# A graph attention layer on one core: TensorE takes the second masks' products one step later

## The chip, the cores and the metric

One core of a Trainium2 chip. The metric is the device time of one launch in microseconds (us), the median of the runs. Three runs of the kernel before took 1816.73, 1818.39 and 1822.62 us.

## What is computed

A graph attention layer over 8192 nodes with 128 features and 4 heads of 32, then ELU, a residual and a layer norm:

```
Wh      = (x @ W.T) as (n, 4, 32)
e[n,h,m] = leaky_relu(score_l[n,h] + score_r[m,h], 0.2)
e       = -inf where adj[n,m] + eye == 0
out     = elu(sum over m of softmax(e)[n,h,m] * Wh[m,h,:])
result  = layernorm(x + out)
```

`adj` is an 8192 x 8192 matrix of zeros and ones in fp32, 256 MB, and is read once.

## The kernel before

The exponential of a leaky ReLU is one of two products of a factor of n and a factor of m, by the sign of score_l + score_r. So the kernel makes two masks of bytes for each pair of tiles of m: one of the edges where the sum is not negative (`bmask`), one of the edges where it is (`cmask`), and multiplies each with its own values (`Wh` times the factor of m, split into three bf16 parts side by side, 99 columns).

**Passes and steps.** A pass (`w`, 16 of them) makes the sums of 16 units of 128 rows for one head (passes 0 to 3 are narrow: 8 units for each of two heads). Each pass has 32 steps (`s`), and a step takes two tiles of m. `q = 32 * w + s` counts all 512. In a step TensorE does 32 matmuls with `bmask` and 32 with `cmask` (both line 396), all accumulated in seven PSUM banks (`psum`): the first three and part of the fourth hold the first masks' sums, the rest the second masks'.

**TensorE** (`step`, lines 384 to 421) does for each q: wait for the values and for the first mask, the first masks' 32 products, signal `half_done`; then, in some steps, `turn_block` (lines 357 to 366: 32 matmuls that pack a block of `adj` into bits); then wait for `c_ready`, the second masks' 32 products, signal `mm_done`. `TURNED` says where the blocks are turned: in 14 steps of pass 0, in every second step of passes 1 to 3, at s = 1, 5, 9, ..., 29 of passes 4 to 11 and nowhere after.

**VectorE** does for each q, in program order: `mask_b(q)` (line 695), part of the compares for q + 1 (line 682), and `mask_c(q)` (line 700), which waits for `mm_done` of step q - 3 since `cmask` has 3 buffers. At s = 0 of a pass it adds up the parts of the pass before (line 706): three banks after `half_done` of its last step, four after `mm_done` of its last step. It waits there in program order, ahead of `mask_b` of s = 1. The first products of the new pass wait for the bank that they open (`bank_free`).

**ScalarE** does the other compares (line 488) three steps ahead, up to six first masks being there (`BR`), and the copies of the turned blocks (line 457).

**SyncE** issues all DMAs on one queue, in program order (lines 284 to 313). `adj` comes in blocks of 2 MB, each as two DMAs of 1 MB (`load_block`, line 217) into two buffers. From pass 2 on the values of a step are read from DRAM into a ring of `VR` = 4 (`load_v`, line 248, 99 KB; line 246 in passes 2 and 3, 198 KB). In iteration q SyncE first issues the block for which the last turned block made room, then the values of step q + 3:

```
284:             loaded, turned = 2, AHEAD
285:             for q in range(Q):
287:                 while loaded < NB and loaded - 1 <= turned:
288:                     load_block(loaded)
292:                 if JUST_MADE * STEPS <= q + VR - 1 < Q:
293:                     load_v(q + VR - 1)
294:                 turned += len(TURNED[q])
```

`load_block(n)` waits for `tr_done` of n - 1 blocks, and `load_v(n)` for `mm_done` of step n - 4, which had the same buffer. So after a turn in step t, the order on the queue is values of t + 3, block, values of t + 4.

Of the kernel before, what the change touches and what calls it, by code (L numbers as in the profile page):

```python
# [6 lines left out]
def gat_kernel(nc, x, adj, W, a_l, a_r, out):  # L7
# [12 lines left out]
    STEPS = NT // 2  # L20
# [9 lines left out]
    EVERY_STEPS = STEPS // NG  # L30
# [10 lines left out]
    JUST_MADE = 2  # L41
# [3 lines left out]
    def narrow(w):  # L45
        return UNITS[w][0][2] != UNITS[w][1][2]
# [9 lines left out]
    def turned_at(q):  # L56

        if q < STEPS:
            return [FIRST_TURNS[q]] if q in FIRST_TURNS else []
        if q < 4 * STEPS:  # L60
            return [] if q % 2 else [QUADS + (q - STEPS) // 2]
        n = 4 * QUADS + (q - 4 * STEPS) // 4
        return [n] if q % 4 == 1 and n < NB else []

    TURNED = [turned_at(q) for q in range(Q)]
# [27 lines left out]

    FINISHED = [(1, range(0, SUB)), (3, range(SUB, JC))] + [(4 * c + 3, range(JC)) for c in range(1, NC)]
    ROWS_DONE = [sum(len(js) for _, js in FINISHED[:e]) for e in range(len(FINISHED) + 1)]

    BR, CR, VR, VS, AH = 6, 3, 4, 3, 3
# [10 lines left out]
    with ctx:  # L108
        def sb(name, shape, dt):
            return ctx.enter_context(nc.sbuf_tensor(name, shape, dt))  # L110

        def sem(name):
            return ctx.enter_context(nc.semaphore(name))
# [7 lines left out]
        bmask = sb("bmask", [P, BR, 2, 2, HALF], fp8)  # L121
        cmask = sb("cmask", [P, CR, 2, 2, HALF], fp8)
# [61 lines left out]
        v_prod, v_hi, v_rest, v_mid, v_lo = (sem(s) for s in ("v_prod", "v_hi", "v_rest", "v_mid", "v_lo"))  # L184
# [4 lines left out]
        v_in = [sem(f"v_in{k}") for k in range(VR)]  # L189
        lrow_in, cmp_act, cmp_dve = [sem("lrow_in0"), sem("lrow_in1")], sem("cmp_act"), sem("cmp_dve")  # L190
        b_ready, c_ready, half_done, mm_done, bank_free = (sem(s) for s in ("b_ready", "c_ready", "half_done", "mm_done", "bank_free"))
# [5 lines left out]
        def wait(eng, s, value):  # L197

            if not (isinstance(value, int) and value <= 0):
                eng.wait_ge(s, value)  # L200
# [119 lines left out]
        @block.tensor  # L320
        def _(pe):
            pe.wait_ge(consts, 1)
            pe.wait_ge(w_in, 16)
            nc.tensor.transpose(psum[:, BANKS - 1, 0:P], w_nat[:, :], identf[:, :]).then_inc(w_tr, 1)
            pe.wait_ge(ablk_done, 1)

            nc.tensor.matmul(psum[:, BANKS - 2, 0:2 * H], w_nat[:, :], ablk[:, :], start=True, stop=True).then_inc(wa_done, 1)
            pe.wait_ge(wt_done, 2)

            def turn_x(g):  # L330
                pe.wait_ge(x_in[g % 4], 16 * (g // 4 + 1))
                wait(pe, x_copied, g - 1)
                for j in range(4):
                    last = nc.tensor.transpose(psum[:, g % 2, j * P:(j + 1) * P], xs[:, g % 4, j], identf[:, :])
                last.then_inc(x_tr, 1)

            def project(g):

                pe.wait_ge(x_copied, g + 1)
                wait(pe, wh_copied, 2 * (g - 1))  # L340
                wait(pe, lc_done, g - 1)
                for j in range(4):
                    last = nc.tensor.matmul(psum[:, 2 + 2 * (g % 2) + j // 2, (j % 2) * WH:(j % 2 + 1) * WH], x_t[:, g % 2, j], w_t[:, :],
                                            start=(j % 2 == 0), stop=True, skip_group_check=True)
                last.then_inc(wh_done, 1)

            def turn_l(c):
                pe.wait_ge(lc_done, 4 * (c + 1))
                wait(pe, lrw_done, c)
                nc.tensor.transpose(psum[0:H * JC, BANKS - 1, 0:P], lcols[:, c], identf[:, :]).then_inc(l_tr, 1)  # L350

            def turn_l_back(c):
                pe.wait_ge(l_copied, c + 1)
                nc.tensor.transpose(psum[:, BANKS - 1, P + c * H * JC:P + (c + 1) * H * JC], l_t[0:H * JC, c],
                                    identf[0:H * JC, 0:H * JC]).then_inc(l_back, 1)

            def turn_block(n):

                pe.wait_ge(a_loaded[n % 2], 32 * (n // 2 + 1))
                wait(pe, evac_done, n)  # L360
                for k in range(BITS):
                    for j in range(SUB):
                        block_hi = abuf[:, n % 2, j, k * P:(k + 1) * P].bitcast(bf16)[:, 1::2]
                        last = nc.tensor.matmul(trp[:, j * P // 2:(j + 1) * P // 2], block_hi, pack[:, k], start=(k == 0 and j == 0), stop=True,  # L364
                                                skip_group_check=True)
                last.then_inc(tr_done, 1)

            for g in range(XG + 1):
                if g < XG:
                    turn_x(g)  # L370
                if g > 0:
                    project(g - 1)
                if g > 4 and g % 4 == 1:
                    turn_l(g // 4 - 1)
                if g > 4 and g % 4 == 2:
                    turn_l_back(g // 4 - 1)
                if g == 13:
                    pe.wait_ge(pack_made, 1)
                    turn_block(0)
            turn_block(1)  # L380
            turn_l(NC - 1)
            turn_l_back(NC - 1)

            def step(q):
                w, s = WHERE[q]

                opened = set()

                def product(mask, u, j, b, values):

                    bank, at = PLACE[(b * 2 + u) * SUB + j]
                    opening = s == 0 and bank not in opened
                    if opening:
                        opened.add(bank)
                        wait(pe, bank_free, BANKS * (w - 1) + bank + 1)
                    return nc.tensor.matmul(psum[:, bank, at * S3:(at + 1) * S3], mask[:, j * P:(j + 1) * P], values,  # L396
                                            start=opening, stop=True, skip_group_check=True)

                def values(u, i, b):
                    if w < JUST_MADE:  # L400
                        return vt[:, q // EVERY_STEPS % VS, u, 2 * (s % EVERY_STEPS) + i, b]
                    at = i * VW + b * S3
                    return vring[:, q % VR, u if narrow(w) else 0, at:at + S3]

                ORDER = [(i, u, j) for i in range(2) for u in range(2) for j in range(SUB)]
                if s == 0:
                    ORDER = [(i, u, j) for u in range(2) for j in range(SUB) for i in range(2)]
                if w < JUST_MADE:
                    pe.wait_ge(v_lo, q // EVERY_STEPS + 1)
                else:  # L410
                    pe.wait_ge(v_in[q % VR], 16 * ((q - JUST_MADE * STEPS) // VR + 1))
                pe.wait_ge(b_ready, q + 1)
                for i, u, j in ORDER:
                    last = product(bmask[:, q % BR, u, i], u, j, 0, values(u, i, 0))
                last.then_inc(half_done, 1)
                for n in TURNED[q]:
                    turn_block(n)
                pe.wait_ge(c_ready, q + 1)
                for i, u, j in ORDER:
                    last = product(cmask[:, q % CR, u, i], u, j, 1, values(u, i, 1))  # L420
                last.then_inc(mm_done, 1)

            pe.wait_ge(wh_copied, 2 * XG)
            pe.wait_ge(lc_done, XG)
            pe.wait_ge(lrw_done, NC)
            for q in range(Q):
                step(q)


        @block.scalar  # L430
# [494 lines left out]
```

## Time and profile before

| | |
|---|---|
| median of 3 runs | 1818.39 us |
| profiled execution, its own time | 1823.02 us |
| its span | 1821.2 us |
| VectorE busy | 95% of the span |
| TensorE busy | 91% |
| ScalarE busy | 89% |
| mean granted TensorE clock | 0.986 |

The span runs from the first to the last instruction of the profiled execution. A busy share is a mean over stages with different limits, so the table alone does not say what sets the time. Matmul ends are modelled, so that neighbouring groups overlap by about 0.16 us; from start to start they are exact.

### The profile page before, as it was taken

How to read it: one execution, taken by the hardware profiler on the slowest of the kernel's cores; microseconds unless marked ns; L12 is line 12 of the kernel's file. 1: busy time of each engine (PE TensorE's matmuls, PEld its weight loads, DVE VectorE, ACT ScalarE, POOL GpSimd, SP SyncE). 2: the span in 40 equal slices, each digit the busy share in tenths (PEclk: the TensorE clock that was granted, in tenths of full speed). 3: DMA queues.
4: the chain of work that ended last, by engine and by line, in shares of the span. 5: the costliest groups of instructions: out<-in, count | busy, mean ns of one | idle time of the engine just before them, and what ended most of it. 6: DMA issues, size and time to landing. Idle time of an engine off the chain costs nothing. (4 is left out here: it accounts for less than half of the span.)

```text
span 1821.2 us, 81366 instructions
## 1 busy us (share of the span) xinstructions
PE 1659.8 (91%) x37067; PEld 1627.4 (89%) x37067; DVE 1734.2 (95%) x1928; ACT 1612.2 (89%) x1217; POOL 24.0 (1%) x34
## 2 busy tenths in 40 slices
PE   6788888889898999999999999999999899999993
PEld 6787887889898999999999999999999899999893
DVE  5999999988988999999999999999999999999996
ACT  4989999789779998998989998998989998998981
POOL 0000000000000100000000100000000100000000
PEclk9899999999999999999999999999999999999997
DMA  8995898999997676576666676666662131121111
GB/s 256 342 341 195 308 311 297 367 334 354 355 323 253 208 241 217 181 237 198 216 211 207 200 238 200 211 209 205 220 194 59 31 95 43 36 57 36 32 36 31
DMA packets 241478, 368.12 MB, mean 202 GB/s; under 512 B 12912, under 2 KB 103408, under 8 KB 239600
## 3 DMA queue, kind: packets, MB, share of 16 engines
q1 hardware_dynamic: 241136, 362.92, 60.7%
q8 instruction: 292, 4.78, 1.1%
q14 instruction: 50, 0.41, 0.1%
HBM read 345.57 MB, written 17.30 MB: 199 GB/s over the span
## 5 line engine op out<-in xcount | busy, mean ns | idle before, releaser
L488 ACT ACTIVATE bmask<-lrow,rtab 128x2048 fp8e4<-128x2048 f32 (+1 forms) x936 | 1483.2, 1661 | 33.1 <-DVE cmask L700 24.1
L396 PE MATMUL psum<-vring,bmask 128*128 128x99 bf16 x14336 | 723.4, 208 | 35.5 <-DVE bmask L695 13.2
L396 PE MATMUL psum<-vring,cmask 128*128 128x99 bf16 x14336 | 718.9, 208 | 37.1 <-DVE cmask L700 21.8
L396 PEld LDWEIGHTS psum<-vring,bmask 128*128 128x128 fp8e4 x14336 | 669.0, 97 | 44.8 <-issue 30.6
L396 PEld LDWEIGHTS psum<-vring,cmask 128*128 128x128 fp8e4 x14336 | 661.6, 98 | 51.9 <-DVE cmask L700 30.7
L700 DVE SCALAR_TENSOR_TENSOR cmask<-acache,bmask 128x1024 int32<-128x1024 int32 x512 | 625.0, 1221 | 27.5 <-PE psum L396 20.6
L695 DVE SCALAR_TENSOR_TENSOR bmask<-acache,bmask 128x1024 int32<-128x1024 int32 x512 | 624.2, 1219 | 0.0
L682 DVE TENSOR_SCALAR bmask<-lrow,rtab 128x2048 fp8e4<-128x2048 f32 (+1 forms) x344 | 357.6, 1055 | 0.0
L457 ACT CAST acache<-trp 128x512 int16<-128x512 f32 x128 | 74.0, 578 | 111.4 <-PE trp L364 111.1
L364 PE MATMUL trp<-pack,abuf 128*128 128x64 bf16 x4096 | 144.1, 194 | 15.9 <-issue 11.1
L364 PEld LDWEIGHTS trp<-pack,abuf 128*128 128x128 bf16 x4096 | 132.8, 99 | 17.6 <-issue 12.3
L396 PE MATMUL psum<-vt,bmask 128*128 128x99 bf16 x2048 | 104.2, 209 | 27.7 <-DVE bmask L695 17.4
L396 PEld LDWEIGHTS psum<-vt,bmask 128*128 128x128 fp8e4 x2048 | 95.9, 98 | 28.8 <-issue 28.5
L396 PE MATMUL psum<-vt,cmask 128*128 128x99 bf16 x2048 | 105.1, 209 | 9.1 <-issue 6.8
L396 PEld LDWEIGHTS psum<-vt,cmask 128*128 128x128 fp8e4 x2048 | 96.2, 98 | 12.5 <-issue 7.8
L706 DVE TENSOR_REDUCE acc<-psum 128x165 f32<-128x495 f32 (+1 forms) x112 | 61.4, 620 | 20.6 <-PE psum L396 20.6
L498 ACT ACTIVATE late<-late,nmr,vrs 128x128 f32<-128x128 f32 x64 | 27.2, 486 | 8.7 <-DVE nmr L796 8.7
L439 ACT COPY acache<-psum 128x256 f32<-128x256 f32 x32 | 10.3, 375 | 23.0 <-DVE acache L579 23.0
L493 ACT ACTIVATE late<-late 128x512 f32<-128x512 f32 x16 | 10.0, 628 | 22.1 <-DVE late L756 22.1
L896 POOL TENSOR_TENSOR vrs<-mv,epsc 128x16 f32<-128x16 f32 (+1 forms) x5 | 4.6, 919 | 1747.8 <-DVE mv L790 1747.8
L627 DVE TENSOR_TENSOR late<-vring,vt 128x1056 f32<-128x1056 f32 x16 | 20.1, 1254 | 2.2 <-ACT vt L460 2.2
L619 DVE TENSOR_TENSOR vring<-acache,vv 128x528 f32<-128x528 f32 x32 | 21.1, 702 | 0.8 <-ACT vv L508 0.8
(62 smaller groups left out, 259.9 us busy)
## 6 DMA issues: line engine op xcount, KB each, us to landing
abuf<-in_adj_dram SPq DMA_DIRECT2D x256, 1024.0 KB, 8.4
vring<-v_scratch SPq DMA_DIRECT2D x384, 99.0 KB, 3.1
lrow<-l_scratch SPq DMA_DIRECT2D x16, 1024.0 KB, 7.8
v_scratch<-vt SPq DMA_DIRECT2D x16, 792.0 KB, 11.1
vring<-v_scratch SPq DMA_DIRECT2D x64, 198.0 KB, 8.2
cmask<-in_x_dram SPq DMA_DIRECT2D x16, 256.0 KB, 4.4
late<-in_x_dram SPq DMA_DIRECT2D x16, 256.0 KB, 4.2
out_dram<-late SPq DMA_DIRECT2D x16, 256.0 KB, 3.5
```

What stands on the lines that cost most here:

```text
L364: last = nc.tensor.matmul(trp[:, j * P // 2:(j + 1) * P // 2], block_hi, pack[:, k], start=(k == 0 and j == 0), stop=True, skip_group_chec ...
L396: return nc.tensor.matmul(psum[:, bank, at * S3:(at + 1) * S3], mask[:, j * P:(j + 1) * P], values, start=opening, stop=True, skip_group_c ...
L439: nc.scalar.copy(wh[:, at:at + 3:2].rearrange("p t (h e) -> p t h e", e=E)[:, :, :, 0:DK], both.rearrange("p t (h d) -> p t h d", d=DK)).t ...
L457: nc.scalar.copy(acache[:, c % 2, half, m].bitcast(i16), trp[:, :]).then_inc(evac_done, 1)
L488: last = nc.scalar.activation(to, rows, ACT.Relu, bias=rtab[:, 2 * s + i, H + h:H + h + 1], scale=BIG, saturate=False)
L498: nc.scalar.activation(zz[:, j], zz[:, j], ACT.Identity, bias=nmr[:, j:j + 1], scale=vrs[:, j:j + 1]).then_inc(y_ready, 1)
L619: last = nc.vector.tensor_tensor(v5[:, :, :, b], w4, vb, ALU.mult)
L627: nc.vector.tensor_tensor(vr, vf, dst[:, :, 0:E], ALU.subtract).then_inc(v_rest, 1)
L682: last = nc.vector.tensor_scalar(to, rows, rtab[:, 2 * s + i, h:h + 1], None, ALU.is_ge, saturate=False)
L695: nc.vector.scalar_tensor_tensor(m, adj_words(q), bit_of(q), m, ALU.bitwise_and, ALU.bitwise_and).then_inc(b_ready, 1)
L700: nc.vector.scalar_tensor_tensor(mask_words(cmask[:, q % CR]), adj_words(q), bit_of(q), mask_words(bmask[:, q % BR]), ALU.bitwise_and, ALU ...
L706: nc.vector.tensor_reduce(acc[:, START[b]:START[b] + n], psum[:, b, 0:n * S3].rearrange("p (i s e) -> p i e s", s=3, e=E), AX.X, ALU.add). ...
```

## The change

TensorE's order alone is altered. For each q it does the first masks' products of q, the turned block of q if there is one, and then the second masks' products of q - 1. In the last step of a pass those of q follow at once; in the first step of a pass there are none. No other engine's program is touched. The reset of `opened` is now by pass and bank.

```diff
-            def step(q):
+            opened = set()
+
+            def branch(q, b):
+
                 w, s = WHERE[q]
...
-                if w < JUST_MADE:
-                    pe.wait_ge(v_lo, q // EVERY_STEPS + 1)
+                if b == 0:
+                    if w < JUST_MADE:
+                        pe.wait_ge(v_lo, q // EVERY_STEPS + 1)
+                    else:
+                        pe.wait_ge(v_in[q % VR], 16 * ((q - JUST_MADE * STEPS) // VR + 1))
+                    pe.wait_ge(b_ready, q + 1)
+                    for i, u, j in ORDER:
+                        last = product(bmask[:, q % BR, u, i], u, j, values(u, i))
+                    last.then_inc(half_done, 1)
                 else:
-                    pe.wait_ge(v_in[q % VR], 16 * ((q - JUST_MADE * STEPS) // VR + 1))
-                pe.wait_ge(b_ready, q + 1)
-                for i, u, j in ORDER:
-                    last = product(bmask[:, q % BR, u, i], u, j, 0, values(u, i, 0))
-                last.then_inc(half_done, 1)
-                for n in TURNED[q]:
-                    turn_block(n)
-                pe.wait_ge(c_ready, q + 1)
-                for i, u, j in ORDER:
-                    last = product(cmask[:, q % CR, u, i], u, j, 1, values(u, i, 1))
-                last.then_inc(mm_done, 1)
+                    pe.wait_ge(c_ready, q + 1)
+                    for i, u, j in ORDER:
+                        last = product(cmask[:, q % CR, u, i], u, j, values(u, i))
+                    last.then_inc(mm_done, 1)
...
             for q in range(Q):
-                step(q)
+                branch(q, 0)
+                for n in TURNED[q]:
+                    turn_block(n)
+                if q % STEPS > 0:
+                    branch(q - 1, 1)
+                if q % STEPS == STEPS - 1:
+                    branch(q, 1)
```

## Rows read from the trace of the kernel before

**Rows 1.** The page: span, then busy us and share of each engine.

```profile
span 1821.2 us, 81366 instructions
PE 1659.8 (91%) x37067; PEld 1627.4 (89%) x37067; DVE 1734.2 (95%) x1928; ACT 1612.2 (89%) x1217; POOL 24.0 (1%) x34
```

**Rows 2.** Busy time by stretch: us, engines, granted clock, DMA share, GB/s.

```profile
560.00:1384.00 824.00, 804.13 (x18424) 796.44 (x18422) 815.03 (x832) 764.74 (x475) 10.83 (x4) 1.00 0.65 208
...
313.00:560.00 247.00, 220.53 (x5128) 216.64 (x5127) 214.93 (x255) 202.61 (x211) 3.15 (x2) 0.99 1.01 345
1384.00:1794.00 410.00, 382.78 (x8200) 369.74 (x8197) 407.08 (x423) 360.56 (x204) 4.92 (x2) 1.00 0.17 47
```

**Rows 3.** Waits, 560 to 1384 us: who waited for whom, us, times, longest.

```profile
PE psum L396 <- issue: 6.6, 11, 1.5
...
DVE acc L706 <- PE psum L396: 5.1, 3, 3.0
```

**Rows 4.** Waits over the whole span, those of VectorE for TensorE.

```profile
DVE cmask L700 <- PE psum L396: 20.6, 20, 1.9
DVE acc L706 <- PE psum L396: 20.6, 7, 5.8
```

**Rows 5.** Timeline of TensorE, steps 169 to 173 (pass 5): start, us, what.

```profile
692.64 1.60 PE L396 MATMUL psum<-vring,bmask 128*128 128x99 bf16 x32
...
695.01 1.59 PE L396 MATMUL psum<-vring,cmask 128*128 128x99 bf16 x32
696.44 1.60 PE L396 MATMUL psum<-vring,bmask 128*128 128x99 bf16 x32
...
705.09 1.60 PE L396 MATMUL psum<-vring,bmask 128*128 128x99 bf16 x32
```

**Rows 6.** Timeline of VectorE in the same stretch, the first masks of three steps.

```profile
694.52 1.22 DVE L695 SCALAR_TENSOR_TENSOR bmask<-acache,bmask 128x1024 int32<-128x1024 int32 x1
...
696.92 1.22 DVE L695 SCALAR_TENSOR_TENSOR bmask<-acache,bmask 128x1024 int32<-128x1024 int32 x1
...
700.39 1.22 DVE L695 SCALAR_TENSOR_TENSOR bmask<-acache,bmask 128x1024 int32<-128x1024 int32 x1
```

**Rows 7.** Timeline of SyncE's queue in pass 5: block, values; then a later block.

```profile
695.21 0.94 SPq L217 DMA_DIRECT2D abuf<-in_adj_dram  x2
696.63 8.97 SPq L248 DMA_DIRECT2D vring<-v_scratch  x4
...
720.50 1.52 SPq L217 DMA_DIRECT2D abuf<-in_adj_dram  x2
```

**Rows 8.** Line 217 alone, the block issued at 695.2 us: its two halves.

```profile
DMA to landing us min/median/max: 5.9/7.4/9.0
```

**Rows 9.** Line 248 alone: values issued at 696.6, at 722.1 and from 1385 us on.

```profile
DMA to landing us min/median/max: 8.3/8.3/8.3
...
DMA to landing us min/median/max: 7.4/7.4/7.4
...
DMA to landing us min/median/max: 1.8/1.9/4.3
```

**Rows 10.** Timeline at the end of pass 4, PE and DVE: sums, first products of pass 5.

```profile
661.72 3.83 DVE L706 TENSOR_REDUCE acc<-psum 128x165 f32<-128x495 f32 x7
...
662.70 1.75 PE L396 MATMUL psum<-vring,bmask 128*128 128x99 bf16 x32
...
666.84 1.33 PE L396 MATMUL psum<-vring,bmask 128*128 128x99 bf16 x26 [0.69 <-DVE bmask L695]
```

**Rows 11.** Pass 2: a block on SyncE's queue, and line 246, the values issued at 351.4 us.

```profile
349.96 0.93 SPq L217 DMA_DIRECT2D abuf<-in_adj_dram  x2
...
DMA to landing us min/median/max: 9.1/9.1/9.1
```

**Rows 12.** A gap after which the clock fell, and a stretch with a gap where not.

```profile
1079.63 2.85 PE L396 MATMUL psum<-vring,bmask 128*128 128x99 bf16 x32 [1.95 <-DMA vring<-v_scratch]
...
180.00:183.40 3.40, 0.95 (x21) 0.81 (x18) 3.40 (x5) 3.40 (x4) 0.00 (x0) 1.00 0.00 0
```

More of the change, by code:

```diff
@@ L382, in _, with product @@
             turn_l_back(NC - 1)
-            def step(q):
+            opened = set()
+            def branch(q, b):
                 w, s = WHERE[q]
-                opened = set()
-                def product(mask, u, j, b, values):
+                def product(mask, u, j, values):
                     bank, at = PLACE[(b * 2 + u) * SUB + j]
-                    opening = s == 0 and bank not in opened
+                    opening = s == 0 and (w, bank) not in opened
                     if opening:
-                        opened.add(bank)
+                        opened.add((w, bank))
                         wait(pe, bank_free, BANKS * (w - 1) + bank + 1)
@@ L397, in product, with values @@
                                             start=opening, stop=True, skip_group_check=True)
-                def values(u, i, b):
+                def values(u, i):
                     if w < JUST_MADE:
```

## The prediction

> **What bounds the kernel now.** I read the page first, for the shares: VectorE is busy 95% of the span and TensorE 91% [rows 1]. Both are near the end of what they can give, so stages decide. The busy time by stretch splits them. From 560 to 1384 us (passes 4 to 11, with turned blocks) VectorE is busy 815 of 824 us, 103.0 us for a pass; from 1384 to 1794 us (no blocks) it is busy 407 of 410 us, 102.5 us for a pass. There VectorE sets the time, blocks or not. From 313 to 560 us (passes 2 and 3) the DMA engines are full, share 1.01 [rows 2]. The waits say how little VectorE loses to TensorE: 20.6 us at the second mask and 20.6 us at the sums in the whole span [rows 4], 5.1 us of it between 560 and 1384 us [rows 3].
>
> Then the timeline of one turn, in pass 5, for how close TensorE is behind. TensorE starts the first products of step 169 at 692.64, then turns a block, starts the second products at 695.01, and those of the next step at 696.44: 2.37 us for products and turn, 1.43 us for a half step. Step 173 starts at 705.09, 12.45 us after 169 [rows 5]. VectorE takes 3.47 us for a step with a compare and 2.40 us for one without [rows 6], so for four steps 3 x 3.47 + 2.40 = 12.8 us. TensorE has 0.35 us to spare in four steps.
>
> The queue has as little. The block is issued at 695.21, when the turn ends, the values of step 173 at 696.63, when the second products of 169 end [rows 7]. The block's second half, issued 0.4 us behind its first, lands at 704.6 [rows 8], the values at 696.63 + 8.3 = 704.9 [rows 9], and TensorE starts step 173 at 705.09. Where no block is ahead the same load lands in 1.9 us (median from 1385 us on) [rows 9]. So the values come when the block ahead of them has come, about 9.7 us after it was issued, and TensorE takes them 0.1 to 0.2 us later. That is the edge of a wait, and the change moves both of its ends.
>
> **The change, part by part.**
>
> *Removed: waits inside a step.* TensorE no longer waits for the second mask right behind the first products. TensorE is not the bound there, so this gives nothing. What hides it is VectorE's own work; with that cover gone it would be worth at most VectorE's waits below.
>
> *Moved: the second products, and with them the signal behind which both DMAs stand.* Take a turn in step t. Now: first products of t, turn, block issued at the turn's end; second products of t, values of t + 4 issued. After: first products of t, turn, second products of t - 1. SyncE stands in iteration t until step t - 1 is done, so only then it issues the values of t + 3 and, behind them, the block; the block no longer goes at the turn's end but a half step and one DMA issue later. The values of t + 4 follow one whole step later and still queue behind the block. I keep 9.7 us from the block's issue to their landing. One issue on that queue costs about 0.45 us (0.94 us for the two of a block) [rows 7]. From the block's issue TensorE has 2.87 us of work per step, and until the first products of t + 4 there are six half steps, 6 x 1.43 = 8.6 us, where there were seven after the issue, 10.0 us.
>
> So the block is issued 0.03 + 0.45 us behind the second products, the values land 9.7 us later, 10.2 us in all, and TensorE has 8.6: it waits 1.6 us. This is a loop, because the next block hangs on the turn behind that wait: first products and turn 2.37, second products 1.59 to their end, 0.03 + 0.45 to the block's issue, 9.7 to the landing, 0.05 to the start = 14.2 us for four steps. VectorE's 12.8 no longer decides. Without the move the same loop is 2.37 + about 0.2 + 9.7 + 0.05 = 12.3 us, under 12.8; that is why it costs nothing today.
>
> *Bounds of 9.7.* The later block goes at 720.50 and the values behind it land at 722.1 + 7.4 = 729.5, 9.0 us later [rows 7, 9]. The lower end is 9.0, loop 13.5. Above, the values of t + 3 now go right ahead of the block; their own transfer could push it by 0.3 us: 10.0, loop 14.5. I take 9.7, as nothing of the block's own path changes.
>
> *The pass end.* In the first step of a pass TensorE has only the first products, and the next ones need the mask that VectorE makes after seven sums. Now at the end of pass 4: sums from 661.72 for 3.83 us, first products at 662.70, the next step's at 666.84 after a 0.69 us wait, with the second products between [rows 10]. After, these come later, and TensorE idles some 2 us. When TensorE is late, VectorE waits for the last second products, then makes four sums (4/7 of 3.83 = 2.2 us) and a mask (1.2): with hand-overs 3.7 us from the last products' end to step 1. From the turn in s = 29 to step 1 of the next pass: 2.37 + 5 x 1.43 + 1.59 + 3.7 = 14.8 us.
>
> *Sum for passes 4 to 11.* Seven loops and one end: 7 x 14.2 + 14.8 = 114.2 us for a pass; eight are 914, less one wait of 1.6 because the last two turns have no block left to load: 912. Now they take 824 [rows 2]: +88 us. TensorE has pauses of its own there, 6.6 us [rows 3]; about a third of a loop has no cover, so +2. An idle end of a pass can take the clock down: the first products after the gap at 1079.63 took 2.85 instead of 1.60 us, while 0.95 us of work in 3.4 us left the clock at 1.00 [rows 12]. For eight ends, 0 to 12 us; I take +4.
>
> *Passes 2 and 3*, a block every second step. The block at 349.96 and the values issued at 351.39 that land 9.1 us later give 10.5 us [rows 11]; the loop is 2.37 + 1.59 + 0.48 + 10.5 + 0.05 = 15.0 us per four steps. The measured mean is 247 / 16 = 15.4 us, with full DMA engines [rows 2], but it has quick and slow stretches, and the quick ones lose. Bounds 0 and, if every four steps lost all of the shift of the issue, 1.43 + 0.45 = 1.9 us, +30 (16 x 1.9). I take +10.
>
> *Passes 0 and 1* have no values on the queue: 0 but for the end, where TensorE is behind. With the ends of passes 2 and 3: 1.4 + 1 + 2 us. *Passes 12 to 15* have no blocks; values land in 1.9 us and TensorE's chain of a pass, 63 x 1.43 + 3.7 = 94 us, stays under VectorE's 102.5: 0. *The end*: the last second products come one half step later against the last mask, but the first three sums go ahead of them: +1.
>
> Sum: 88 + 2 + 4 + 10 + 4 + 1 = **+109 us**. The profiled execution took 1823.0 us, 1.8 more than its span, so it would be 1932; it stands 4.6 us above the median, and from 1818.4 I forecast **1927 us**.
>
> A rule of the Trainium skill speaks against the queueing. "DMA: Bandwidth & Descriptors", section "Queues, rings and completion order", says that a later transfer may finish its write before an earlier one, and that completion is not in order per issuing engine. By it the values could land ahead of the block, and the sum would lose its 88. This case's trace shows them 0.3 us behind it, at 704.9 against 704.6.
>
> **The rivals.**
>
> *The values pass the block, or the wait stays covered.* What speaks for it: VectorE has hidden all else. Then only pass ends and small terms remain, 1 to 10 us: 1824. It needs the landing at or below 8.3 us from the block's issue (loop 12.8), and the shortest that I cite is 9.0. Chance 0.08.
>
> *Faster.* The first masks' sums need only the last first products, and these now end a half step before the rest. If the queue holds nothing up, VectorE's waits at the sums shrink by up to 1.43 us in each of seven [rows 4], 10 us, less 1 at the end: 1809. It decides from a landing at 8.3 us or less and pass ends that cost nothing. Chance 0.03.
>
> *The clock.* If each wait of 1.6 us also took TensorE's clock down, products behind it would cost 1.25 us more (2.85 against 1.60) [rows 12]: 55 x 1.25 = 69 on top, 1996. Against it: the emptier stretch at 180 us kept its clock. Chance 0.09.
>
> **How the numbers follow.** The loop has 0.80. With its terms at the low end (9.0: 55 x -0.7 = -39; passes 2 and 3 at 0; clock 0) it gives 1874, at the high end (+0.3 each, +16; passes 2 and 3 +19; clock +8) 1970. A range of 1868 to 1970 holds nearly all of the 0.80. The measurement tells 0.3%, 5.5 us, from no change; the first rival's 0.08 falls about evenly on both sides of that. Faster 0.03, same 0.05, slower 0.92.
>
> **What would show it.** Passes 4 to 11 at about 114 us each and 12 to 15 still at 102; in each; seven waits of TensorE for the values of 1.4 to 1.8 us; the block issued behind a load of values, a half step after the turn; VectorE waiting for TensorE at the second mask. If those passes stay near 103 us, or TensorE's waits are for masks, the step "the values land 9.7 us after the block's issue" is wrong.

## The result and the profile after

The changed kernel takes 1978.5 us (median of 4 runs, 1964.7 to 1981.4) against 1820.4 us (4 runs) for the kernel before: 1.084 times the time, 95% interval 1.081 to 1.087. The forecast was 1927 us within 1868 to 1970. The direction and the mechanism held; the size is 158 us where 109 were forecast, and the time lies 8.5 us above the range.

From the page of the changed kernel: the span, the busy times, the chain that ended last by engine and by line, and two of the costliest groups with the idle time before them.

```profile
span 1979.6 us, 81366 instructions
PE 1706.6 (86%) x37067; PEld 1675.4 (85%) x37067; DVE 1738.6 (88%) x1928; ACT 1614.8 (82%) x1217; POOL 21.8 (1%) x34
...
PE 38%; DMA 29%; DVE 11%; issue 9%; ACT 3%; SPq 1%; DVEq 0%; POOLq 0%; ACTq 0%; POOL 0%
...
L397 PE MATMUL psum<-vring,bmask 128*128 128x99 bf16 x14336 | 742.8, 211 | 178.8 <-DMA vring<-v_scratch 138.0
...
L707 DVE SCALAR_TENSOR_TENSOR cmask<-acache,bmask 128x1024 int32<-128x1024 int32 x512 | 624.8, 1220 | 183.1 <-PE psum L397 178.8
```

VectorE works as long as before (1738.6 against 1734.2 us [rows 1]), so its share falls from 95% to 88%. Two waits of similar size stand out: TensorE before the first masks' products, for the loads of values, 138.0 us; VectorE before the second mask, for TensorE, 178.8 us. They may be one delay seen twice: TensorE is late, and VectorE, with three buffers for the second mask, is held behind it. Which of the two comes first is what the experiments had to show.

The stretches that answer to [rows 2] are passes 4 to 11, passes 12 to 15, and passes 2 and 3. Columns: stretch, its length, busy us of PE, PEld, DVE, ACT, POOL, granted clock, DMA share, GB/s.

```profile
582.00:1545.90 963.90, 843.68 (x18434) 833.96 (x18435) 820.39 (x834) 767.62 (x476) 8.56 (x4) 0.96 0.56 177
...
1542.00:1953.00 411.00, 381.70 (x8202) 374.24 (x8199) 406.81 (x422) 359.11 (x203) 4.92 (x2) 0.99 0.17 47
...
313.00:578.00 265.00, 227.96 (x5133) 223.09 (x5131) 218.52 (x261) 204.85 (x212) 3.15 (x2) 0.96 0.96 320
```

Passes 4 to 11 went from 824 to 964 us, 140 of the 158. Passes 2 and 3 became 16 us longer (262.9 against 246.8 us from their first products to the first products of pass 4; the stretches of the table are cut a little wider). Passes 12 to 15, with the same new order and no blocks, take what they took. The mean granted clock is 0.96 where TensorE waits, in passes 2 to 11. TensorE's and VectorE's waits in passes 4 to 11, in us, times and longest (before, VectorE waited there for TensorE 5.1 us, at the sums [rows 3]):

```profile
DVE cmask L707 <- PE psum L397: 132.1, 70, 5.4
PEld psum L397 <- DMA vring<-v_scratch: 126.8, 62, 3.4
PE psum L397 <- DMA vring<-v_scratch: 111.9, 59, 3.3
```

A loop is the four steps from the first products of a turn's step to those of the next turn's step. One of them, steps 173 to 177 of pass 5, on TensorE (timeline), with the starts that [rows 5] shows for steps 169 to 173, and the turn:

```profile
747.50 1.61 PE L397 MATMUL psum<-vring,bmask 128*128 128x99 bf16 x32 [1.43 <-DMA vring<-v_scratch]
748.96 1.09 PE L364 MATMUL trp<-pack,abuf 128*128 128x64 bf16 x32
749.89 1.59 PE L397 MATMUL psum<-vring,cmask 128*128 128x99 bf16 x32
751.31 1.60 PE L397 MATMUL psum<-vring,bmask 128*128 128x99 bf16 x32
...
761.72 1.61 PE L397 MATMUL psum<-vring,bmask 128*128 128x99 bf16 x32 [1.64 <-DMA vring<-v_scratch]
```

and on SyncE's queue:

```profile
737.51 0.32 SPq L248 DMA_DIRECT2D vring<-v_scratch  x1
737.87 0.99 SPq L217 DMA_DIRECT2D abuf<-in_adj_dram  x2
740.38 11.45 SPq L248 DMA_DIRECT2D vring<-v_scratch  x4
751.87 1.16 SPq L217 DMA_DIRECT2D abuf<-in_adj_dram  x2
```

The second products of step 172 end at 749.89 + 1.59 = 751.48; then the values of step 176 are issued, at 751.51 (the last of the four in the third line), and the block at 751.87, 4.37 us after the start at 747.50. It was 2.57 us (692.64 to 695.21 [rows 5, 7]). From 747.50 to 761.72 are 14.22 us, the 14.2 of the forecast. But the loop before it, from step 169 on, is longer:

```profile
731.95 1.99 PE L397 MATMUL psum<-vring,bmask 128*128 128x99 bf16 x32 [2.12 <-DMA vring<-v_scratch]
733.74 1.91 PE L364 MATMUL trp<-pack,abuf 128*128 128x64 bf16 x32
735.46 2.02 PE L397 MATMUL psum<-vring,cmask 128*128 128x99 bf16 x32
737.32 1.60 PE L397 MATMUL psum<-vring,bmask 128*128 128x99 bf16 x32
```

It takes 15.55 us. The same three groups need 5.37 us (731.95 to 737.32) instead of 3.81 (747.50 to 751.31), 1.56 more, because the clock was at half (granted clock 0.50 in the first row, 1.00 in the second):

```profile
733.00:736.40 3.40, 3.40 (x57) 3.40 (x54) 1.83 (x2) 0.72 (x2) 0.00 (x0) 0.50 0.02 5
747.50:751.00 3.50, 3.50 (x89) 3.50 (x90) 2.38 (x3) 0.91 (x2) 0.00 (x0) 1.00 0.06 14
```

Measured in this way over the 55 loops that lie within a pass and have a block: the mean loop is 15.10 us, 14.50 for the 31 with the full clock and 15.92 for 23 with the half clock (one is between). The block's issue to its last landing takes 9.70 us in the mean (9.22 before), and 8.7 to 11.1 from loop to loop; the values land 0.34 us behind it. So TensorE's wait is not one number either: 1.87 us in the mean, 0.8 to 3.3 from loop to loop.

### The profile page after: what moved, and what is told of

The parts are those of the page before. It is cut to its first block, busy times and chain, and to the rows that moved or that the text cites. A ratio compares the mean times of both kernels' runs of the same rounds, so it can differ in the third digit from the quotient of the medians.

```text
span 1979.6 us, 81366 instructions
## 1 busy us (share of the span) xinstructions
PE 1706.6 (86%) x37067; PEld 1675.4 (85%) x37067; DVE 1738.6 (88%) x1928; ACT 1614.8 (82%) x1217; POOL 21.8 (1%) x34
## 4 chain that ended last, share of the span: by engine, by line
PE 38%; DMA 29%; DVE 11%; issue 9%; ACT 3%; SPq 1%; DVEq 0%; POOLq 0%; ACTq 0%; POOL 0%
PE psum L397 33%; DMA vring<-v_scratch 28%; DVE bmask L702 6%; PE trp L364 5%; ACT bmask L495 3%; DVE acc L713 1%; DVE cmask L707 1%; DMA v_scratch<-vt 1%; DVE vring L626 0%; DVE bmask L689 0%; SPq L217 0%; DVE vt L639 0%; DVE late L634 0%; DVE st L790 0%; ACT late L505 0%
## 5 line engine op out<-in xcount | busy, mean ns | idle before, releaser
L397 PE MATMUL psum<-vring,bmask 128*128 128x99 bf16 x14336 | 742.8, 211 | 178.8 <-DMA vring<-v_scratch 138.0
L397 PEld LDWEIGHTS psum<-vring,bmask 128*128 128x128 fp8e4 x14336 | 685.7, 99 | 199.4 <-DMA vring<-v_scratch 156.1
L707 DVE SCALAR_TENSOR_TENSOR cmask<-acache,bmask 128x1024 int32<-128x1024 int32 x512 | 624.8, 1220 | 183.1 <-PE psum L397 178.8
L397 PEld LDWEIGHTS psum<-vring,cmask 128*128 128x128 fp8e4 x14336 | 670.5, 98 | 6.8 <-issue 6.7
L364 PE MATMUL trp<-pack,abuf 128*128 128x64 bf16 x4096 | 162.6, 203 | 11.9 <-DMA abuf<-in_adj_dram 6.9
L364 PEld LDWEIGHTS trp<-pack,abuf 128*128 128x128 bf16 x4096 | 152.3, 105 | 13.1 <-DMA abuf<-in_adj_dram 7.3
L467 ACT CAST vt<-vring 128x1056 bf16<-128x1056 f32 x16 | 17.8, 1110 | 6.2 <-DVE vring L626 6.2
```

The costliest lines, as they stand in the source:

```text
L467: nc.scalar.copy(vt[:, n % VS].rearrange("p u t b e -> p (u t b) e")[:, :, e:e + E], src).then_inc(done, 1)
L707: nc.vector.scalar_tensor_tensor(mask_words(cmask[:, q % CR]), adj_words(q), bit_of(q), mask_words(bmask[:, q % BR]), ALU.bitwise_and, ALU ...
```

## The experiments

Theory Q: the values of step t + 4, issued behind the block of the turn in step t, come only when the block has come; the block goes later, and TensorE waits. Rival M: what holds the kernel is that the second products, and so the release of the second mask's buffers, come later. Times below are medians; in brackets the ratio to the kernel before with its interval.

**A fifth buffer for the values**, in the changed kernel.

```diff
-    BR, CR, VR, VS, AH = 6, 3, 4, 3, 3
+    BR, CR, VR, VS, AH = 6, 3, 5, 3, 3
```

and SyncE begins these loads in the same step as before. The values of step t + 4 then go ahead of the block, and those behind it are for step t + 5. 

> The changed kernel with five buffers for the values instead of four, nothing else. Theory Q (the values of step t + 4 queue behind the block and TensorE waits for them): with a fifth buffer the same load has two more half steps, 11.5 us against a landing at about 10.5, so the waits for the values go, passes 4 to 11 come back to 102 to 104 us and the whole to 1815 to 1835. Rival M (the second products' signal comes half a step later, and VectorE, with three buffers for the second mask, is held at them: 179 us of such waits stand in the changed kernel's trace): the fifth buffer for the values changes nothing of that, and the time stays near 1978.

1833.3 us (1.006, 1.004 to 1.008). Passes 4 to 11 as one stretch, and the waits in it:

```profile
565.20:1390.50 825.30, 801.94 (x18434) 796.90 (x18435) 816.39 (x833) 765.49 (x476) 10.83 (x4) 1.00 0.65 207
```

```profile
PE psum L399 <- DVE bmask L704: 21.7, 19, 2.0
DVE acc L715 <- PE psum L399: 4.9, 8, 1.0
```

Not one wait for values or at the second mask is left in the list of that stretch, though the second products and their signal stand where they stand in the change, and the second mask has three buffers as before. Rival M falls: VectorE's 178.8 us were the echo. The block is still issued 4.36 us (median) after the start of a loop and still takes 9.70 us to land, so the block's own path is unchanged; only the time that TensorE has is longer.

**SyncE alone, TensorE's order untouched**, in the kernel before: the block waits for the end of the turn's whole step.

```diff
                 wait(sp, tr_done, n - 1)
+                if after is not None:
+                    sp.wait_ge(mm_done, after)
...
-                    load_block(loaded)
+                    load_block(loaded, after=q if 4 * STEPS < q else None)
```

> The kernel before, TensorE's order untouched; only SyncE, from pass 4 on, waits until the turn's whole step is done before it issues the block, so a half step later and right ahead of the values of t + 4. Theory Q: that alone makes the same loop, 2.37 + 1.59 + 0.03 + about 10 + 0.05 = 14.1 us and, with the clock falling in some, 14.5 to 15; passes 4 to 11 take 112 to 120 us, the whole 1900 to 1950, without a product moved. Rival M (the late second products themselves): no change, 1820.

1884.2 us (1.034, 1.032 to 1.037). Not a product was moved, and 53 us of the loss in passes 4 to 11 are here (877 against 824 us). Its waits for values (TensorE's, passes 4 to 11), and the two starts of one loop:

```profile
PE psum L398 <- DMA vring<-v_scratch: 66.3, 59, 1.8
```

```profile
639.49 1.61 PE L398 MATMUL psum<-vring,bmask 128*128 128x99 bf16 x32 [1.83 <-DMA vring<-v_scratch]
...
653.25 1.61 PE L398 MATMUL psum<-vring,bmask 128*128 128x99 bf16 x32 [1.19 <-DMA vring<-v_scratch]
```

13.76 us; the mean of the 55 is 13.73: 4.05 to the block's issue, 9.29 to its landing, 0.33 to the values', 0.05 to the products. The run lies below the 1900 to 1950 that I expected, and the difference to the change's 15.10 says from what: 0.32 is the issue of the values that go ahead of the block in the change, 0.41 the later landing, and the rest, 0.64, the clock, which here never fell (1.00 in the stretch).

```profile
570.10:1447.10 877.00, 807.18 (x18437) 795.72 (x18434) 817.23 (x833) 767.11 (x476) 10.84 (x4) 1.00 0.60 195
```

**Work in the idle time**, for the clock: the change with 24 products into an unused place ahead of each wait.

```diff
             for q in range(Q):
+                if 4 * STEPS <= q < 12 * STEPS and q % 4 == 1 and q % STEPS > 1:
+                    fill(q)
                 branch(q, 0)
```

> The changed kernel, and in passes 4 to 11, just ahead of the wait for the values of s = 5, 9, ..., 29, 24 more products into a place of a bank that nobody reads (about 1.1 us of work where TensorE now idles 1.5 us or more). Its output is that of the changed kernel. Theory Q with the clock term (in 23 of 55 loops TensorE's clock was at half after the wait, and first products, turn and second products took 1.56 us more): idle stretches get short, few of them take the clock down, loops fall from a mean of 15.1 to 14.5 us, the whole by 25 to 36 us to about 1947. Rival W (the long loops come from elsewhere, the clock is only their companion): the same or, for added work, slower, 1978 to 2000.

1955.5 us (1.073, 1.071 to 1.076), 23 us less, with 56 x 1.1 = 62 us of work added. The stretch 4 to 11, and one filled place:

```profile
579.50:1520.00 940.50, 872.43 (x19777) 862.41 (x19778) 819.95 (x833) 769.78 (x477) 8.56 (x4) 0.99 0.57 182
```

```profile
752.28 1.22 PE L430 MATMUL psum<-vring 128*128 128x99 bf16 x24
754.03 1.61 PE L398 MATMUL psum<-vring,bmask 128*128 128x99 bf16 x32 [0.53 <-DMA vring<-v_scratch]
```

The clock stands at 0.99 instead of 0.96 and fell 5 times instead of 25; the mean loop is 14.70 us. TensorE's idle time became shorter, the landing did not (9.74 us). So the clock was a cost of its own: 0.40 us of a loop came back. The 23 us are a little less than the 25 to 36 expected; five falls stay, and the block lands no sooner.

**The new order in passes 4 to 11 alone.**

```diff
-                if q % STEPS > 0:
+                later = 4 * STEPS <= q < 12 * STEPS
+                if later and q % STEPS > 0:
                     branch(q - 1, 1)
-                if q % STEPS == STEPS - 1:
+                if not later or q % STEPS == STEPS - 1:
                     branch(q, 1)
```

> The new order in passes 4 to 11 alone; the others as before. Theory Q: passes 4 to 11 keep their 139 us, passes 0 to 3 give back 15 to 20: 1955 to 1965. Rival E (much of the loss is at starts and ends and in the narrow passes, where TensorE's new order leaves it without second products): under 1930.

1955.3 us (1.074, 1.069 to 1.079). Passes 4 to 11 take 956 us; passes 2 and 3 are back at 245 us. The loss sits where the forecast had it.

**The block first**, at the turn's end and ahead of the values of t + 3.

```diff
+                if w >= 4:
+                    turned += len(TURNED[q])
                 while loaded < NB and loaded - 1 <= turned:
                     load_block(loaded)
...
-                turned += len(TURNED[q])
+                if w < 4:
+                    turned += len(TURNED[q])
```

> The changed kernel with the block, from pass 4 on, issued at the turn's end and ahead of the values of t + 3, as far as it can go forward on the queue. By theory Q it is now the values of t + 3 that stand right behind the block: 2.57 us to the issue, about 9.7 to their landing, then one step of 2.87 us to the next turn's step: a loop of 15.2 us at the full clock, 0.7 longer than the 14.5 of the changed kernel, so passes 4 to 11 get 0 to 40 us slower and the whole 1980 to 2020, with the long waits at s = 4, 8, ... instead of 5, 9, .... If instead the block's late issue as such were the cause, this kernel would be back at 1820 to 1840.

2053.2 us (1.128, 1.125 to 1.130). The block's issue is 2.57 us (median) after the start again, as before the change, and the kernel is the slowest of all. One wait, at s = 16, four steps after the one at s = 12 (762.53 us) and not at 17, and on SyncE's queue the block of the turn at s = 13 with the values behind it:

```profile
779.45 2.26 PE L400 MATMUL psum<-vring,bmask 128*128 128x99 bf16 x32 [2.78 <-DMA vring<-v_scratch]
781.51 2.54 PE L400 MATMUL psum<-vring,cmask 128*128 128x99 bf16 x32
```

```profile
769.54 0.94 SPq L217 DMA_DIRECT2D abuf<-in_adj_dram  x2
770.97 3.21 SPq L248 DMA_DIRECT2D vring<-v_scratch  x2
```

The wait moved to the values that now stand right behind the block, as theory Q has it. The whole lies beyond the 2020 that I gave, by the clock: 0.93 in passes 4 to 11, 40 falls. Loops at full clock take 14.6 us, less than the 15.2 that I worked out; those with a fall take about 17.

**Smaller blocks**, every issue and wait kept.

```diff
+                    if part == 1 and n >= 4 * QUADS + 2:
+                        rows = adj[rows_of(c, half), m * BITS * P:(m + 1) * BITS * P][0:P]
+                        sp.dma_start(abuf[:, n % 2, SUB - 1:SUB], ...).then_inc(a_loaded[n % 2], 16)
+                        continue
```

> The changed kernel; from block 66 on, so in passes 4 to 11, the second DMA of a block brings one tile of rows instead of four (1.25 instead of 2 MB in all), and three row tiles of those blocks keep what the buffer held. All else, every issue and every wait, stands. If the block's transfer is what the values of t + 4 wait for, they land some 2.4 us sooner, within the 8.6 us that TensorE has, the waits go, and the whole is 1830 to 1850. If it is the place of the issue, or the second products' signal, passes 4 to 11 stay near 963 us.

1846.7 us (1.013, 1.012 to 1.015). The block lands 7.10 us after its issue instead of 9.70, passes 4 to 11 (here from 584.3 to 1412.4, first products of their second steps) take 828 us, and few waits for values are left from 561 to 1400 us:

```profile
PE psum L401 <- DMA vring<-v_scratch: 5.2, 4, 2.5
```

The block goes as late as in the change, the signals stand as in the change, and the loss in these passes is gone with a part of the bytes: what the values wait for is the block's transfer. Most of the 25 us that this kernel still loses lie in passes 0 to 3, which the edit does not touch. Its pass 2 took 142 us instead of the change's 134 (from second step to second step); I have no explanation for that.

**The values on a queue of their own**: the same loads, issued by GpSimd.

```diff
-                if JUST_MADE * STEPS <= q + VR - 1 < Q:
-                    load_v(q + VR - 1)
...
+            for q in range(Q):
+                if JUST_MADE * STEPS <= q + VR - 1 < Q:
+                    load_v(q + VR - 1)
```

> The changed kernel with the loads of values issued by GpSimd on its own queue, in the same order and behind the same waits; SyncE then issues the block when the turn ends. Theory Q, as far as it is one queue's order: the values no longer stand behind the block, TensorE does not wait, passes 4 to 11 come back to 102 to 105 us, the whole 1820 to 1840. Rival B (it is the block's bandwidth, shared by all queues, that delays the values): the values still land 7 to 9 us after issue when a block is under way, and passes 4 to 11 stay at 112 us or more, the whole above 1900.

1904.6 us (1.047, 1.045 to 1.048): nearly what I gave to rival B, with passes 4 to 11 at 111 us each. A block of pass 5 is issued at 738.67 us. Behind it the values of s = 16 (GpSimd's queue), with their time to landing, and TensorE's start:

```profile
740.36 0.54 POOL L895 DMA_DIRECT2D vring<-v_scratch  x1 [3.26 <-PE psum L382]
```

```profile
DMA to landing us min/median/max: 7.1/7.1/7.1
```

```profile
747.54 0.66 PE L382 MATMUL psum<-vring,bmask 128*128 128x99 bf16 x11 [1.74 <-DMA vring<-v_scratch]
```

On their own queue they land at 747.5, 0.8 us ahead of the block's end (748.3), and in the mean of the 55 loops 1.6 us ahead of it. But they still take 6.3 us in the mean (7.1 here); with no block under way, in passes 12 to 15, the same load took 2.5 us in this kernel. Passes 4 to 11 take 890 us against 824: about half of the loss stays.

Against the change this run moves the block's issue too, to the turn's end. Against the run with the block first it does not: both issue the block 2.57 us (median) into the loop, and the values of t + 3 1.5 to 1.7 us behind it. There the values took 8.1 us on the block's queue, here 6.3 us on another. So the place on the queue is worth about 1.8 us of a landing, and the larger part of the delay, about 4 us, comes with a block under way, on either queue.

**The same two edits on the kernel before.** The fifth buffer: 

> The kernel before with five buffers for the values, nothing else. If TensorE's waits for values (10 us in the whole span, nearly all in passes 2 and 3) are on the path, they go: passes 2 and 3 give back up to 8 us, 1812 to 1818. If those stretches are bound by the full DMA engines, as their share of 1.01 has it, nothing moves: 1821. Passes 4 to 11 stay at 824 us by both.

1818.1 us (0.9988, 0.9979 to 0.9997), 0.1% and so hardly a gain. In its one trace passes 4 to 11 take 819.5 instead of 824.2 us, and passes 2 and 3 are no quicker (249.5 against 246.8 us). I had expected it the other way round.

GpSimd's queue: 

> The kernel before with the loads of values on GpSimd's queue. By theory Q it has no waits there to lose in passes 4 to 11 (824 us stay); in passes 2 and 3 TensorE's 10 us of waits for values may go or not: 1812 to 1822. Rival (GpSimd's own way of issuing costs landing time or takes something from VectorE): slower than 1825.

1826.7 us (1.004, 1.002 to 1.005): above the 1812 to 1822 that I expected and within what I had given to the rival, over 1825. In its trace passes 4 to 11 lose nothing (822 us), and passes 2 and 3 take 256 us instead of 247. Why GpSimd's queue costs time there is not shown.

**The first step of a pass**: the change with five buffers, and TensorE takes the second products of s = 0 at once.

```diff
-                if q % STEPS > 0:
+                if q % STEPS > 1:
                     branch(q - 1, 1)
-                if q % STEPS == STEPS - 1:
+                if q % STEPS in (0, STEPS - 1):
                     branch(q, 1)
```

> The changed kernel with five buffers for the values, and in the first step of a pass the second products follow at once, so that TensorE has work while VectorE makes the sums; from the second step on they are deferred as in the change. If the 0.6% that the changed order still costs with five buffers is the idle time of TensorE at the 15 pass ends (half a step, 1.43 us each, where TensorE is the one behind), this comes to 1815 to 1822; if it is anything else in the order, it stays at 1828 to 1835.

1830.8 us (1.005, 1.004 to 1.006). Nothing came back. The 0.6% that the new order costs even with values in time are not TensorE's idle half step at the start of a pass.

For passes 4 to 11, where the changed kernel with five buffers takes 825.3 us and the old order with five buffers 819.5, the traces say where it lies. The loops within a pass are as long in both (12.65 and 12.68 us); the four steps across a pass end take 14.67 against 13.66 us. In the changed order VectorE makes three sums and then waits for the last second products; in the old order it makes all seven in one run. The end of pass 4, the changed order with five buffers, then the old one with five:

```profile
663.35 1.83 DVE L715 TENSOR_REDUCE acc<-psum 128x165 f32<-128x495 f32 x3
665.71 2.10 DVE L715 TENSOR_REDUCE acc<-psum 128x165 f32<-128x495 f32 x4 [0.54 <-PE psum L399]
```

```profile
662.89 3.83 DVE L708 TENSOR_REDUCE acc<-psum 128x165 f32<-128x495 f32 x7
```

At the end of a pass TensorE still has the second products of the last two steps to do, and the run above leaves that as it is: it has the same waits (5.5 us in these eight passes, against 0.4 in the old order). No run removed them, so this is read from traces and not tested. The cost in passes 0 to 3 (1 us in the trace with five buffers, which is of the fastest of its eight runs, 1826 us; 5 us in that of this last run) stays open.

## Why the prediction was right in kind and too small

- **What bounds it before**: right. VectorE sets passes 4 to 15, and passes 12 to 15 did not move.
- **"The values land 9.7 us after the block's issue", the lost half step, the loop**: right in kind. TensorE waits at the forecast places, and loops with the full clock take 14.50 us against the forecast 14.2. But one landing time for all loops gave waits of 1.4 to 1.8 us; with landings that differ by 2.4 us the waits were 0.8 to 3.3. The end of a pass was sized right: what is left of the 963.9 us after 55 loops, 963.9 - 55 x 15.10 = 133 us, is about nine groups of four steps (eight pass ends and the one without a block), 14.8 each. The seven ends that lie wholly inside measure 14.96 against the forecast 14.8.
- **The landing**: the term was mis-sized by 0.3 us. I kept 9.7 "as nothing of the block's own path changes" and named 0.3 for the values right ahead of the block as the upper bound. The upper bound was it: 9.70 + 0.34 = 10.04 us. Where values are issued on the queue right ahead of the block (the change, the fifth buffer) it lands in 9.70 us, where not (kernel before, late block, block first) in 9.22 to 9.29. 55 x 0.34 = 19 us.
- **The clock**: the step that failed. The sum put it at 4 us (0 to 12), at pass ends alone, and at nothing in the loops; "each wait takes it down" was a rival with a chance of 0.09, against which I held one emptier stretch that kept its clock. Neither came: 23 of the 55 loops had the fall, 1.56 us each, 36 us. That one stretch [rows 12] showed that a fall need not come, and not that it will not. With the clock as forecast and the landing as measured, the time would have been inside the range.
- **Passes 2 and 3**: +16 us against +10, within the bounds of 0 and 30.
- **The balance** of passes 4 to 11: 140 us against the forecast 88 + 2 + 4 = 94, so 46 are missing. The landing gives 19; the clock 36, less the 4 that stood in the sum; and the block's issue came 0.07 us sooner in each loop, which takes 4 off. Together 47. Passes 0 to 3 with their ends: 19 us against 14.
- **The range**: its upper end took the clock at 12 us. With the fall as a share of the loops between none and all, 0 to 86 us (55 x 1.56), it would have reached past 2000.
- **The rule of the Trainium skill on completion** ("DMA: Bandwidth & Descriptors", "Queues, rings and completion order"), by which a later transfer may finish first: this case does not bear it out for one queue. The values never landed ahead of the block on the same queue; they came behind it by 0.20 us at the least and 0.34 in the mean, in 55 of 55. On another queue they did, in 54 of 55, by 1.6 us in the mean.

## What to carry to other kernels

Where an engine's signal gates a DMA queue, moving the signal moves all that stands behind it in program order; look for the small load that is issued right behind a large one, and count the work that covers it. Cover that ends about 0.3 us after the landing, as here, looks like no cost in every list of waits; here a block issued 1.5 us later and nothing else (4.05 against 2.57 us into the loop) cost 63 us. One more buffer for the small load was worth 145 us in the changed kernel and hardly anything (0.1%) in the kernel before; and where a change creates regular waits of TensorE, its clock belongs in the sum as a term with a share, not as a rival.

## What I had not expected of the hardware

- TensorE's granted clock went to half after idle times of 1.4 to 3.3 us in the changed kernel (25 falls in passes 4 to 11), while some two dozen others of 1.5 to 2.5 us left it alone. In the kernel with the late block, whose 59 waits for values in passes 4 to 11 are of 1.8 us at most, it never fell there. A fall cost 1.56 us here.
- 2 MB blocks landed 9.70 us after issue where 99 KB had been issued 0.4 us ahead of them on the same queue, and 9.2 to 9.3 us where not. The same 99 KB behind a block took 6.5 to 8.9 us instead of 1.9, and on another queue still 5.0 to 7.7.
- Within one queue the values behind a block never landed ahead of it in this study. The least distance in the nine kernels that issue both on SyncE's queue is 0.19 us (95 pairs in each trace).
